# Differential attention on one core: five PSUM banks for five groups of transposes, scores as three rounded products

## The reference, cut to what matters

```python
def _L1_attn_ref(x, Wq, Wk, Wv, Wo, lq1, lk1, lq2, lk2):
    q = (x @ Wq).reshape(B, S, 2, h, dh)
    k = (x @ Wk).reshape(B, S, 2, h, dh)
    v = (x @ Wv).reshape(B, S, 2, h, dh)
    ...
    s1 = jnp.einsum('bshd,bthd->bhst', q1, k1) * scale
    s2 = jnp.einsum('bshd,bthd->bhst', q2, k2) * scale
    s1 = jnp.where(causal, s1, neg_inf)
    s2 = jnp.where(causal, s2, neg_inf)
    a1 = jax.nn.softmax(s1, axis=-1)
    a2 = jax.nn.softmax(s2, axis=-1)
    o = jnp.einsum('bhst,bthd->bshd', a1, v1) - lam * jnp.einsum('bhst,bthd->bshd', a2, v2)
    o = o.reshape(B, S, h * dh) * (1.0 - LAMBDA_INIT)
    return o @ Wo
```

## Time and profile before

| | us |
|---|---|
| median of 3 runs | 1255.46 (1252.87 to 1256.94) |
| time of the profiled execution | 1253.41 |
| its span, first to last instruction | 1252.1 |
| TensorE busy | 1133.1 (90%) |
| VectorE busy | 925.4 (74%) |
| ScalarE busy | 644.3 (51%) |
| GpSimd busy | 444.5 (35%) |

### The profile page before, as it was taken

One profiled execution on the slowest core, in us unless ns is written; L12 is line 12 of the kernel. 1 busy time (PEld: TensorE's weight loads), 2 busy tenths in 40 slices (PEclk: granted clock), 3 DMA queues, 4 the chain that ended last, 5 costly groups with the idle time before them and its releaser, 6 DMA issues.

```text
span 1252.1 us, 21979 instructions
## 1 busy us (share of the span) xinstructions
PE 1133.1 (90%) x7102; PEld 777.9 (62%) x7102; DVE 925.4 (74%) x3272; ACT 644.3 (51%) x1668; POOL 444.5 (35%) x720
## 2 busy tenths in 40 slices
PE   0967769999998849999999999999999999999997
PEld 0866625666666635666666666666666666656676
DVE  1597968999989458777777777777777878756767
ACT  0220035555555326666666666666666677654441
POOL 0426331333313024434343334444343455333310
PEclk9997988999999879999999999999999999999999
DMA  9100030000000000000000000000000000000000
GB/s 272 38 1 1 1 102 1 1 1 2 1 2 1 1 1 1 1 2 1 1 2 1 2 1 1 1 2 2 1 1 1 2 2 1 2 1 4 9 10 15
DMA packets 19952, 15.26 MB, mean 12 GB/s; under 512 B 2432, under 2 KB 18816, under 8 KB 19712
## 3 DMA queue, kind: packets, MB, share of 16 engines
q1 hardware_dynamic: 19840, 13.86, 3.8%
HBM read 12.81 MB, written 1.05 MB: 11 GB/s over the span
## 4 chain that ended last, share of the span: by engine, by line
PE 73%; DVE 14%; issue 6%; ACT 3%; POOL 3%; DMA 1%; SPq 1%; DVEq 0%; POOLq 0%
PE bank L1454 13%; PE bank L1448 12%; PE bank L1484 11%; PE bank L1405 8%; PE bank L1753 5%; PE bank L1774 4%; PE bank L969 4%; PE bank L1425 3%; PE bank L1433 3%; DVE prob L1244 2%; PE bank L954 2%; DVE xm_e L719 1%; ACT prb L1508 1%; PE bank L929 1%; PE bank L947 1%
## 5 line engine op out<-in xcount | busy, mean ns | idle before, releaser
L1534 POOL TENSOR_SCALAR prb<-prb,rnorm 128x512 f32<-128x512 f32 (+3 forms) x512 | 273.5, 555 | 374.3 <-DVE rnorm L1608 374.3
L1508 ACT ACTIVATE prb<-prb,negmax 128x512 f32<-128x512 f32 (+3 forms) x512 | 280.4, 549 | 112.9 <-DVE negmax L1590 112.9
L1590 DVE CUSTOM_DVE_ANT_0 prb<-bank,mask 128x512 f32<-128x512 f32 (+3 forms) x512 | 218.8, 484 | 23.5 <-PE bank L1448 23.5
L1454 PE MATMUL bank<-ident,prb 128*128 128x128 f32 x1280 | 170.2, 276 | 8.3 <-DVE prbT L1601 3.4
L1454 PEld LDWEIGHTS bank<-ident,prb 128*128 128x128 f32 x1280 | 138.6, 141 | 41.0 <-issue 25.7
L1448 PE MATMUL bank<-kT,qT 64*128 64x512 f32 (+3 forms) x1024 | 160.6, 451 | 0.2 <-DVE negmax L1590 0.2
L1484 PE MATMUL bank<-prbT,vv 128*64 128x512 f32 (+3 forms) x1024 | 151.9, 439 | 0.0
L1516 ACT ACTIVATE prbT<-bank 128x512 f32<-128x512 f32 x128 | 76.5, 598 | 112.9 <-PE bank L1454 112.9
L1599 DVE COPY prbT<-bank 128x512 f32<-128x512 f32 x128 | 88.5, 691 | 36.0 <-PE bank L1454 32.0
L1484 PEld LDWEIGHTS bank<-prbT,vv 128*64 128x64 f32 x1024 | 63.4, 136 | 83.1 <-issue 83.1
L1448 PEld LDWEIGHTS bank<-kT,qT 64*128 64x128 f32 x1024 | 90.7, 186 | 28.4 <-issue 11.9
(11 more groups left out here) (427 smaller groups left out, 2018.5 us busy)
## 6 DMA issues: line engine op xcount, KB each, us to landing
x<-in_x SPq DMA_DIRECT2D x2, 512.0 KB, 6.2
ew2T<-in_ew2T SPq DMA_DIRECT2D x1, 1024.0 KB, 8.4
ew<-in_ew SPq DMA_DIRECT2D x1, 1024.0 KB, 5.7
wq<-in_Wq SPq DMA_DIRECT2D x2, 512.0 KB, 5.3
wk<-in_Wk SPq DMA_DIRECT2D x2, 512.0 KB, 7.6
wv<-in_Wv SPq DMA_DIRECT2D x1, 1024.0 KB, 8.2
out<-res SPq DMA_DIRECT2D x16, 64.0 KB, 1.5
wmod<-in_wmod SPq DMA_DIRECT2D x2, 384.0 KB, 6.2
```

The costliest lines, as they stand in the source:

```text
L1454: last = T.transpose(into[:, at + (qc - kc) * P:at + (qc - kc + 1) * P], prb[j % 2][:, i, p_at[qc] + kc * P:p_at[qc] + (kc + 1) * P], iden ...
L1508: A.activation(v, v, ACT.Exp, scale=-1.0, bias=negmax[j % 2][:, place[qc], i:i + 1], accum_out=rowsum[j % 2][:, place[qc], i:i + 1]).then_ ...
L1534: last = G.tensor_scalar(v, v, rnorm[j % 2][:, place[qc], i:i + 1], 1.0, ALU.mult, ALU.mult)
L1590: V.tensor_tensor_reduce(prb[j % 2][:, i, p_at[qc]:p_at[qc] + (qc + 1) * P], s_of(j, s, i, qc), mask[:, (NT - 1 - qc) * P:S], 1.0, LARGEST ...
```

## The change

It does four things.

- **Scores.** `scores` makes each block in three rounded passes (high·high, high·low, low·high) where there was one plain product.
- **High and low halves.** ScalarE now makes the high halves of both keys (new, L1510 after) and queries (in place of the old copy). VectorE makes both low halves, as projected value minus high half, in a new step `remainders`; the copy of the keys is gone from it. `remainders` stands behind `project_v` in the order, and waits for ScalarE's high halves. `BK` and `BQ` now come free when the low halves are made.
- **Banks.** The five groups of transposes use five banks: 4 in bank 2, 0 in bank 3, 1 in `BM`, 2 in bank 4, 3 in bank 5 (in the last unit `BK` and `BQ`).
- **Memory.** The halves take twice the room, and the experts' `res` and `abel` of one batch are moved. In the experts' part three waits are added on the copies of the last units' transposes.

```diff
-        TURN_BANK = {4: bank[2], 0: bank[3], 1: BM, 2: bank[2], 3: bank[3]}
+        def turn_bank(j, part):
+            last = (BK, BQ) if j == UNITS - 1 else PAIR[0]
+            return {4: PAIR[2][0], 0: PAIR[2][1], 1: BM, 2: last[0], 3: last[1]}[part]
...
             for j in range(LEAD):
                 project_k(j)
                 project_q(j)
+                remainders(j)
...
                 if j + 3 < UNITS:
                     project_v(j + 3)
+                if j + LEAD < UNITS:
+                    remainders(j + LEAD)
...
             def scores(j, s):
-                q, k = qT[j % LEAD], kT[j % LEAD]
+                (q_hi, q_lo), (k_hi, k_lo) = qT[j % LEAD], kT[j % LEAD]
...
                 for qc in STEPS[s]:
-                    for i in range(2):
-                        r = slice(DH * i, DH * i + DH)
-                        last = T.matmul(s_of(j, s, i, qc), q[r, qc * P:(qc + 1) * P], k[r, 0:(qc + 1) * P], start=True, stop=True)
+                    for n, (q, k) in enumerate(((q_hi, k_hi), (q_hi, k_lo), (q_lo, k_hi))):
+                        for i in range(2):
+                            r = slice(DH * i, DH * i + DH)
+                            last = T.matmul(s_of(j, s, i, qc), q[r, qc * P:(qc + 1) * P], k[r, 0:(qc + 1) * P], start=(n == 0), stop=(n == 2))
...
         def attention_scalar(ahead):
+            def project_k(j):
+                A.wait_ge(at_proj, 2 * j + 1)
+                if j >= LEAD:
+                    A.wait_ge(at_s, 6 * (j - LEAD + 1))
+                A.activation(kT[j % LEAD][0], BK[:, :], ACT.Copy).then_inc(at_khi, 1)
...
-                A.activation(qT[j % LEAD], BQ[:, :], ACT.Copy, scale=-DH ** -0.5).then_inc(at_qk, 1)
+                A.activation(qT[j % LEAD][0], BQ[:, :], ACT.Copy, scale=-DH ** -0.5).then_inc(at_qhi, 1)
...
         def attention_vector(ahead):
-            def project_k(j):
-                V.wait_ge(at_proj, 2 * j + 1)
+            def remainders(j):
+                V.wait_ge(at_khi, j + 1)
                 if j >= LEAD:
                     V.wait_ge(at_s, 6 * (j - LEAD + 1))
-                V.tensor_copy(kT[j % LEAD], BK[:, :]).then_inc(at_kk, 1)
+                hi, lo = kT[j % LEAD]
+                V.tensor_tensor(lo, BK[:, :], hi.bitcast(F32), ALU.subtract).then_inc(at_kk, 1)
+                V.wait_ge(at_qhi, j + 1)
+                hi, lo = qT[j % LEAD]
+                V.scalar_tensor_tensor(lo, BQ[:, :], -DH ** -0.5, hi.bitcast(F32), ALU.mult, ALU.subtract).then_inc(at_qk, 1)
...
             def widen(b, j):
...
+                    T.wait_ge(*((at_pta, 2 * UNITS), (at_ptv, 3 * UNITS))[j])
```

More of the change, by code:

```diff
@@ L284, in build @@
         UNITS = PER * B
-        at = Region(ARENA - 2048)
+        SCORED = ARENA - 4096
+        at = Region(SCORED)
         LEAD = 2
-        qT = [at.take(f"qT{i}", [P, S]) for i in range(LEAD)]
-        kT = [at.take(f"kT{i}", [P, S]) for i in range(LEAD)]
+        qT = [[at.take(f"qT{i}{n}", [P, S], F32R) for n in ("hi", "lo")] for i in range(LEAD)]
+        kT = [[at.take(f"kT{i}{n}", [P, S], F32R) for n in ("hi", "lo")] for i in range(LEAD)]
         at = Region(0)
@@ L305, in build @@
         at = Region(RAW)
-        res, abel = ([at.take(f"{n}{b}", [P, NT, D]) for b in range(B - 1)] for n in ("res", "abel"))
-        res.append(last_res)
-        abel.append(last_abel)
+        res, abel = ([at.take(f"{n}{b}", [P, NT, D]) for b in range(B - 2)] for n in ("res", "abel"))
         xhat1 = [at.take(f"xhat1_{k}", [P, NT, D]) for k in range(3)]
@@ L312, in build @@
         dots = at.take("dots", [P, NT, D])
-        assert at.at <= ARENA - 2048
+        assert at.at <= SCORED
+        for n, rows_of in (("res", res), ("abel", abel)):
+            rows_of.append(at.take(f"{n}{B - 2}", [P, NT, D]))
+        res.append(last_res)
+        abel.append(last_abel)
         stats1 = sb("stats1", [P, NT, 6])
@@ L349, in build @@
             "xm_norm_done", "xm_all_done", "xm_ready", "xm_ps", "xm_old", "rot_ps", "rot_kept", "ew2_ps", "ew2_kept"))
-        at_proj, at_qk, at_kk, at_vps, at_v, at_s, at_max, at_exp, at_rn, at_norm = (sem(n) for n in (
-            "at_proj", "at_qk", "at_kk", "at_vps", "at_v", "at_s", "at_max", "at_exp", "at_rn", "at_norm"))
+        at_proj, at_qhi, at_khi, at_qk, at_kk, at_vps, at_v, at_s, at_max, at_exp, at_rn, at_norm = (sem(n) for n in (
+            "at_proj", "at_qhi", "at_khi", "at_qk", "at_kk", "at_vps", "at_v", "at_s", "at_max", "at_exp", "at_rn", "at_norm"))
         at_w, at_h = sem("at_w"), sem("at_h")
@@ L1329, in last_scores, with attention_order @@
                 read(j + 2, 0, 1)
-        def attention_order(split_w, split_h, project_q, project_k, project_v, project_out, scores, read, turn, normalise, apply, collect, ahead):
+        def attention_order(split_w, split_h, project_q, project_k, remainders, project_v, project_out, scores, read, turn, normalise, apply, collect, ahead):
             for n in range(3):
@@ L1445, in scores @@
                 for qc in STEPS[s]:
-                    for i in range(2):
-                        r = slice(DH * i, DH * i + DH)
-                        last = T.matmul(s_of(j, s, i, qc), q[r, qc * P:(qc + 1) * P], k[r, 0:(qc + 1) * P], start=True, stop=True)
-                        if qc == STEPS[s][-1]:
-                            last.then_inc(at_s, 1)
+                    for n, (q, k) in enumerate(((q_hi, k_hi), (q_hi, k_lo), (q_lo, k_hi))):
+                        for i in range(2):
+                            r = slice(DH * i, DH * i + DH)
+                            last = T.matmul(s_of(j, s, i, qc), q[r, qc * P:(qc + 1) * P], k[r, 0:(qc + 1) * P], start=(n == 0), stop=(n == 2))
+                            if n == 2 and qc == STEPS[s][-1]:
+                                last.then_inc(at_s, 1)
             def turned(j, i, kc, at, into):
@@ L1459, in turn @@
                 T.wait_ge(at_norm, 3 * j + (2, 2, 3, 3, 1)[part])
-                into = TURN_BANK[part]
+                into = turn_bank(j, part)
                 claim(into)
@@ L1491, in attention_tensor @@
             T.wait_ge(ew2_kept, E1 * HC // 4 + 1)
-            yield from attention_order(skip, skip, project_q, project_k, project_v, project_out, scores, skip, turn, skip, apply, skip, ahead)
+            yield from attention_order(skip, skip, project_q, project_k, skip, project_v, project_out, scores, skip, turn, skip, apply, skip, ahead)
         def attention_scalar(ahead):
+            def project_k(j):
[3 more added lines that the diff above has]
+                A.activation(kT[j % LEAD][0], BK[:, :], ACT.Copy).then_inc(at_khi, 1)
             def project_q(j):
                 A.wait_ge(at_proj, 2 * j + 2)
-                if j >= LEAD:
-                    A.wait_ge(at_s, 6 * (j - LEAD + 1))
-                A.activation(qT[j % LEAD], BQ[:, :], ACT.Copy, scale=-DH ** -0.5).then_inc(at_qk, 1)
+                A.activation(qT[j % LEAD][0], BQ[:, :], ACT.Copy, scale=-DH ** -0.5).then_inc(at_qhi, 1)
             def read(j, s, i):
@@ L1515, in turn @@
                         A.wait_ge(at_pv, j)
-                    A.activation(prbT[:, part // 2, 0:S], TURN_BANK[part][:, :], ACT.Copy).then_inc(at_pta, 1)
+                    A.activation(prbT[:, part // 2, 0:S], turn_bank(j, part)[:, :], ACT.Copy).then_inc(at_pta, 1)
             def apply(j):
@@ L1523, in apply @@
                     A.activation(oT, BO[:, :], ACT.Copy).then_inc(at_o, 1)
-            yield from attention_order(skip, skip, project_q, skip, skip, skip, skip, read, turn, skip, apply, skip, ahead)
+            yield from attention_order(skip, skip, project_q, project_k, skip, skip, skip, skip, read, turn, skip, apply, skip, ahead)
         def attention_gpsimd(ahead):
@@ L1536, in normalise @@
                         last.then_inc(at_norm, 1)
-            yield from attention_order(*[skip] * 9, normalise, skip, skip, ahead)
+            yield from attention_order(*[skip] * 10, normalise, skip, skip, ahead)
         def attention_vector(ahead):
@@ L1610, in attention_vector @@
             V.wait_ge(qkv_in, QKV_IN)
-            yield from attention_order(split_w, split_h, skip, project_k, project_v, project_out, skip, read, turn, normalise, skip, collect, ahead)
+            yield from attention_order(split_w, split_h, skip, skip, remainders, project_v, project_out, skip, read, turn, normalise, skip, collect, ahead)
         HALF = E1 * HC
@@ L1718, in turn @@
                     T.wait_ge(at_max, 8 * UNITS)
+                    T.wait_ge(at_pta, 2 * (UNITS - 1))
+                    T.wait_ge(at_ptv, 3 * (UNITS - 1))
                 T.wait_ge(mx_xhat, 2 * b + 2)
```

4 lines of the change are left out of this document (2 added, 2 removed).

## The result

The changed kernel takes 1249.48 us (median of 7 runs, 1247.33 to 1250.64) against 1256.21 us of the kernel before (7 runs). The ratio is 0.9947, with a 95% interval of 0.9931 to 0.9963: some 6.7 us faster, a third of the 20 us forecast. The profiled execution took 1249.02 us, its span is 1247.7.

The account below looks back on a forecast made before the run. TensorE was taken to set the pace. The terms -18.6 - 11.5 + 8.4 + 1.5 = -20.2 took the profiled 1253.4 to 1233.2 us; 2.05 more for the median gave 1235, range 1218 to 1256.

Parts of the forecast that it names:

- The scores: TensorE's scores in three rounded passes instead of one plain product save 0.29 us a turn, -18.6 us over 64 turns.
- rival 2: In the scores, a rounded pass of 128 columns costs 0.217 us instead of 0.111: +20, total 0, 1255 us; chance 0.10.
- rival 5: Weight loads of the scores' rounded passes are not hidden: +56 us for the scores, 1296 us in all; chance 0.04.
- rival 6: The scores' rounded passes on the two halves of the rows run one after the other: +101, 1341 us; chance 0.05.
- The banks: New banks remove the fourth transpose group's wait for VectorE's copy: 0.18 us a turn, -11.5 us over 64 turns.
- Rival 4: Changing the transposes' banks brings nothing, the idle 0.21 us not being due to the copy: -9, 1246 us; chance 0.05.
- The third group in long turns: Third transpose group waits 0.44 us for the output sum, against 0.17: 0.27 given back in 31 long turns, +8.4 us.
- Rival 3: Low halves come early enough that the third transpose group never waits in long turns: -34, 1221 us; chance 0.08.
- The short turn just fits: In short turns VectorE is free at S+10.10 (S: scores' start), before the next reads at S+10.2: 0.1 us to spare.
- The subtractions: VectorE's two added subtractions for the low halves take 0.684 us each, 0.61 from start to start.
- Rival 1: VectorE's subtractions cost 0.848 us, each adding 0.16, in long and short turns: total -3, 1252 us; chance 0.13.
- Ends: Outside the regular turns, +1.2 us at the start and +0.5 at the end, taken as +1.5 in all.

## Why the prediction was wrong

The direction was right; the size was three times too large. One term is missing, the extra tasks of VectorE, and it costs 20 us; that the banks gave 6 more than forecast hides a part of it.

- **The scores.** Forecast -0.29 a turn from rounding. The stage went from 2.44 to 2.11 (708.69 to 710.80), of which the banks have 0.08; so rounding gives 0.25. The narrow passes are 0.11 apart (709.38, 709.49, 709.60), the floor of the weight loads that I took, but for the first, which is followed after 0.06 (709.32); 384 columns are 0.17 to 0.18 apart and 256 0.12, the first 0.17. The six passes of 128 and 256 columns take 0.69 together. Rivals 2, 5 and 6 are refuted. The count of four passes for true FP32 (Trainium skill, FP8 and Floating Point Precision, TensorE Precision Notes) would have given three quarters of the stream. The trace comes near it for 512 columns (three passes 0.70, a plain product 0.86) and disagrees for 128 (0.28 against 0.22), where the loads decide. With the rule that a load overlaps a running matmul only in another row group (Trainium skill, TensorE: Matmul & The Clock Gate, Part 3, The mechanism) the trace disagrees here too: with an unhidden load of 0.11 a pass the stage would be near 3.3 by the sum of rival 5, not 2.11.
- **The banks.** Forecast -0.18 a turn, measured -0.26 (short) and -0.30 (long), about -17.4 over 62 turns instead of -11.5. Rival 4 is refuted. Missed was the 0.08 in the scores, which I had counted among what stays, and that the transposes of the long turn gain some 0.03 more than those of the short one.
- **The third group in long turns.** Forecast +0.27; the transposes of a long turn take 2.70 (705.99 to 708.69), with the banks alone 2.47: +0.23. Right in a regular long turn. Rival 3 is refuted, since the wait is there.
- **The short turn just fits.** Right for a regular one: 9.02. This is the place where the sum then broke (below).
- **The subtractions.** Forecast 0.684 and 0.61 from start to start; measured 0.69 and 0.68, 0.6 apart. Rival 1 is refuted.
- **Ends.** From the first projection to the first score 8.83 went to 9.92, +1.1 against +1.2. The granted clock was 0.79 of full speed on average in both stretches. From the last scores' start to the end of the span 152.06 went to 151.93; the +0.5 forecast there is not seen.
- **The step that failed** is in the paragraph on the short turn: "It just fits, with 0.1 to spare." I read one short and one long turn and took all to be like them, in the 0.1 for the short turns as in the 0.27 "in each of 31 long turns". Behind the subtractions, in the same queue place, VectorE has nine splits of weights, three of activations, three collects and four moments, two instructions or more each, against 0.1 us of room. I had written that "everything more on VectorE or ahead of the high halves lands on TensorE", and the sum has no term for what was already there. It measured 0.86 for a split of activations, 1.27 for a collect (whose two instructions take 1.45 to the next start, 657.30 to 658.75) and 1.3 to 1.5 for moments, each in the long turn behind it. The 14 long turns that got longer cost +15.8 where the sum had them, at the measured regular gain, at -4.3: 20 us, of which turn 60 is 0.7. Put right, the sum is: the 31 short turns -16.4 in all, the 17 regular long ones -5.4, the 14 others together +15.8, and -1.9 in entry 0, which makes -7.8 over the 63 distances (unrounded); with +1.1 from the first projection to the first score it is -6.7. The medians differ by 6.7 too; that they agree so closely is in part luck, since the stretch ahead of the attention varies by some us (last section).

## What to carry to other kernels

When a change uses up an engine's idle time in a regular iteration, list every irregular task of that engine (per batch, per chunk of weights, the next stage's early work) and price the iterations that hold one separately: there the cover was already in use. Look for the delay in the iteration behind the task, too. A step that makes one engine wait for another inside its queue loses the waiting time as cover, so the first thing to try is an earlier place for what it waits for, here two ScalarE instructions ahead of two others, worth 24 us. And test the parts of a change one by one: here one part alone beat the whole, and the other alone was a loss.

## What was not expected of the hardware

The stretch ahead of the attention takes different times in different executions of the same kernel. The first projection of the kernel with the banks alone began at 449.99 us in one profile and at 454.48 in another:

```profile
449.99 0.77 PE L1408 MATMUL bank<-h0hi,wk0hi 128*128 128x512 f32 x1 [5.25 <-DVE h0lo L1556]
```

```profile
454.48 0.77 PE L1408 MATMUL bank<-h0hi,wk0hi 128*128 128x512 f32 x1 [5.25 <-DVE h0lo L1556]
```

From entry 1 on the turns of the attention repeat to 0.02 us in both. Entry 0 does not (11.40 and 12.35), nor does the way from the first projection to the first score (8.87 and 10.25). For the profiled executions of before and after the same point lies at 451.6 and 454.1, which hides 2.5 us of the gain if the two spans are compared. A difference of a few us in one program is better read from distances inside the stretch that was changed. A part of the variation goes with TensorE's clock. Ahead of the first projection the granted clock was 0.5 of full speed (the level of 1.2 GHz) for 50.8 us in the first of the two profiles and for 55.3 us in the second. From there to the first score it was 0.79 and 0.67 on average: the rounded products of 512 columns come 0.43 apart at the lower level and 0.23 at the upper, and the higher level came back near 453.8 in the first and 460.6 in the second. Why it fell and rose at different places is not shown; the two runs were on different chips.
